# Attention probabilities of batch 0: turned by way of HBM and VectorE instead of on TensorE

## The reference

```python
xn = layernorm(x)
q, k, v = split(xn @ w_qkv.T + b_qkv)
probs = softmax(q @ k.T / sqrt(512))          # 1024 x 1024 for each batch
s = (probs @ v) @ w_out.T + b_out
# gate: a mixture of 8 experts on the same xn, best 2 of 8 for each token
topk_vals, topk_idx = top_k(xn @ router_w + router_b, 2)
h = silu(xn @ expert_w[e] + expert_b[e])      # for the two chosen experts
g = silu(norm_w * rms_normalise(xn + (sum of weighted h) @ proj_w + proj_b))
out = x + s * g
```

## Time and profile before

| | |
|---|---|
| median of 3 runs | 507.1 us (506.06 to 507.46) |
| the profiled execution | 505.39 us, span of its instructions 503.7 us |
| TensorE, VectorE, ScalarE, GpSimd busy | 488.0, 299.7, 206.7, 202.6 us |
| granted TensorE clock | 0.999 of full speed |
| DMA | 104.22 MB, mean 207 GB/s |

### The profile page before, as it was taken

How to read it: one execution, slowest core, us unless ns; L and a number is a source line. 1 busy time by engine, 2 the same in 40 slices (tenths; PEclk the granted TensorE clock), 3 DMA queues, 4 the chain that set the end, 5 groups by cost and what they waited for, 6 DMA issues and landing times.

```text
span 503.7 us, 7293 instructions
## 1 busy us (share of the span) xinstructions
PE 488.0 (97%) x2234; PEld 397.2 (79%) x2235; DVE 299.7 (60%) x452; ACT 206.7 (41%) x300; POOL 202.6 (40%) x288
## 2 busy tenths in 40 slices
PE   4999999999999999799999999999999999999996
PEld 2678686888888888688888888878888888888884
DVE  2556252576422535688888889763676645667452
ACT  1166373142212333854444444323454362525550
POOL 3044310004887835860000000754477772466134
PEclk9999999999999999999999999999999999999999
DMA  7863999912688489998985666987253451331202
GB/s 261 303 231 145 379 384 366 394 43 84 220 310 298 159 248 285 307 272 247 287 219 189 188 202 181 311 287 276 65 148 114 150 175 62 116 95 62 84 33 94
DMA packets 68364, 104.22 MB, mean 207 GB/s; under 512 B 5728, under 2 KB 29808, under 8 KB 68336
## 3 DMA queue, kind: packets, MB, share of 16 engines
q1 hardware_dynamic: 55120, 67.13, 42.1%
q0 software_dynamic: 7360, 25.19, 14.6%
q10 hardware_dynamic: 5856, 11.54, 6.5%
HBM read 60.32 MB, written 43.52 MB: 206 GB/s over the span
## 4 chain that ended last, share of the span: by engine, by line
PE 90%; DMA 3%; issue 2%; ACT 2%; POOL 1%; DVE 1%; SPq 1%; ACTq 0%
PE ab L1451 20%; PE ab L1453 20%; PE ab L1452 20%; PE sc L1451 6%; PE sc L1453 6%; PE sc L1452 6%; PE tp L1457 4%; PE sc L1468 3%; DMA raw<-in_expert_w 2%; PE tp L1502 2%; DMA raw_o<-in_w_out_t 1%; PE sc L1531 1%; PE ab L1476 1%; ACT W L941 1%; PE sc L1534 1%
## 5 line engine op out<-in xcount | busy, mean ns | idle before, releaser
L720 POOL DMA_INDIRECT y<-y_scratch,pos x32 | 31.1, 972 | 107.2 <-DMA y_scratch<-yt_so 92.5
L1451 PE MATMUL ab<-W,st_h 128*128 x156 | 60.9, 390 | 2.7 <-DVE st_l L1189 2.7
L1453 PE MATMUL ab<-W,st_l 128*128 x156 | 60.7, 389 | 0.0
L1452 PE MATMUL ab<-W,st_h 128*128 x156 | 60.7, 389 | 0.0
L703 POOL DMA_INDIRECT rows_scratch<-xb,pos x32 | 31.2, 976 | 52.4 <-DVEq L1185 44.2
L1451 PE MATMUL sc<-xt_h,t_h 128*128 128x512 f32 x128 | 50.3, 393 | 0.0
L1453 PE MATMUL sc<-xt_h,t_l 128*128 128x512 f32 x128 | 50.0, 390 | 0.0
L1452 PE MATMUL sc<-xt_l,t_h 128*128 128x512 f32 x128 | 49.8, 389 | 0.0
L932 ACT CAST st_h<-tp 128x512 fp32r<-128x512 f32 x39 | 22.9, 588 | 42.8 <-PE ab L1453 34.1
L1245 DVE TENSOR_REDUCE small<-sc 128x1 f32<-128x1024 f32 x16 | 19.6, 1224 | 29.8 <-PE sc L1453 25.4
L1451 PEld LDWEIGHTS ab<-W,st_h 128*128 128x128 f32 x156 | 29.3, 188 | 9.6 <-issue 3.5
(11 more groups left out here) (261 smaller groups left out, 1219.0 us busy)
## 6 DMA issues: line engine op xcount, KB each, us to landing
rows_scratch<-xn ACTq DMA_DIRECT2D x3, 3328.0 KB, 19.3
xb<-in_expert_w POOLq DMA_DIRECT2D x6, 1024.0 KB
xn<-rows_scratch SPq DMA_DIRECT2D x48, 128.0 KB, 3.0
xg<-rows_scratch SPq DMA_DIRECT2D x44, 128.0 KB
y_scratch<-yt_own SPq DMA_DIRECT2D x20, 256.0 KB, 2.6
y_scratch<-yt_so SPq DMA_DIRECT2D x19, 256.0 KB, 2.8
rows_scratch<-xs SPq DMA_DIRECT2D x16, 256.0 KB, 6.0
xb<-rows_scratch SPq DMA_DIRECT2D x16, 256.0 KB, 6.2
```

The costliest lines, as they stand in the source:

```text
L720: pool.indirect_dma_start(y[:, q, :], None, y_d, bass.IndirectOffsetOnAxis(pos[:, GB * s + p:GB * s + p + 1], 0))\
L1451: nc.tensor.matmul(dst, lh, rh, start=start, stop=False)
L1452: nc.tensor.matmul(dst, lh, rl, start=False, stop=False)
L1453: return nc.tensor.matmul(dst, ll, rh, start=False, stop=stop)
```

## The change

For the tiles 0 to 6 of batch 0 the eight transposes on TensorE go. ScalarE writes exp with the columns in another order, to one of three buffers in turn (`prob`, and memory of `xn` or `yt_own`, which are idle then). SP stores the 128 x 1024 tile (512 KB) to `p_scratch` in HBM (`store_prob`), waits for it to land, and loads it back with four DMAs of 128 KB in another order of rows (`load_prob`). VectorE turns 32 x 32 blocks of it into `tp` with two transposes (`p_turn`). Tile 7 is still turned on TensorE.

Around that, the queues are written out in a new order. TensorE makes four blocks of scores before the first attention block, the key weights of the second half follow the first attention block, and from then on an attention block is three tiles behind its scores. VectorE reads attention results and row maxima ahead of turns in its loop. The positions are computed before `texp`, which has its own semaphore `assigned`. SP asks for the raw weights of experts 3 and 4 one behind the other after the last scores, ahead of the pair loads; ScalarE casts expert 3 before the last `pt_split` and expert 4 before `g_split(0)`; the projection's raw weights are asked for later.

```diff
+    p_d = nc.dram_tensor("p_scratch", (GB, P, S), F32).ap()
+    p_q = p_d.rearrange("j (r s) (a f) -> j a s r f", r=4, a=4)
...
+        probs = tuple(prob[:, :] if j % 2 == 0 else xn_flat if j < QB else yt_flat for j in range(GB))
+        quarters = tuple(xs[:, 2 * n:2 * n + 2, :].rearrange("p a n -> p (a n)") for n in range(2))
...
+            def store_prob(j):
+                sp.wait_ge(exp_done, 2 + j + 1)
+                sp.dma_start(p_d[j], probs[j], max_dma_last_dim=4 * D).then_inc(p_out[j % 2], 16)
+
+            def load_prob(j):
+
+                sp.wait_ge(p_out[j % 2], 16 * (j // 2 + 1))
+                if j >= 2:
+                    sp.wait_ge(p_turned, j - 1)
+                for a in range(4):
+                    sp.dma_start(quarters[j % 2][32 * a:32 * (a + 1), :].rearrange("p (r f) -> p r f", r=4),
+                                 p_q[j, a, :, :, :]).then_inc(p_in[j % 2], 16)
...
+            sp.wait_ge(t_done, G)
+            for j in range(QB):
+                store_prob(j)
+                load_prob(j)
+            store_s(0)
+            for g in range(GB, GB + 4):
+                load_to_send(g)
+            for j in (QB, QB + 1):
+                store_prob(j)
+                load_prob(j)
+                store_s(j - 3)
+                for g in range(GB + 4 + 2 * (j - QB), GB + 6 + 2 * (j - QB)):
+                    load_to_send(g)
+            store_prob(GB - 2)
+            load_prob(GB - 2)
+            store_s(3)
+
+            sp.wait_ge(s_done, GB)
+            load_raw(sp, 3)
+            load_raw(sp, 4)
+            for g in range(GB):
+                sp.wait_ge(sent[g], 64)
+            load_pair(0, 0)
+            store_s(4)
+            load_pair(2, 1)
+            load_bias(0)
+            load_bias(1)
+            store_s(5)
+            load_next(4, 0)
+            load_bias(2)
+            load_bias(3)
+            store_s(6)
+            store_s(7)
+            load_next(6, 1)
...
+            def pt_split(j):
+                if j < GB - 1:
+                    act.wait_ge(p_turned, j + 1)
+                else:
+                    act.wait_ge(ptr_done, 1)
+                if j >= 2:
+                    act.wait_ge(ab_full, U["a", 0, j - 2] + 1)
...
+            def exp_0(j):
+                act.wait_ge(mx, j + 1)
+                if j >= 2:
+                    act.wait_ge(p_out[j % 2], 16 * (j // 2))
+                out, whole = probs[j], sc[:, j % 2, :, :].rearrange("p m n -> p (m n)")
+                if j < GB - 1:
+                    out = out.rearrange("p (a c q) -> p c a q", a=4, q=32)
+                    whole = whole.rearrange("p (c a q) -> p c a q", a=4, q=32)
...
+            act.wait_ge(zero_in, 48)
+            exp_0(1)
+            early_high(0)
+            pt_split(0)
+            exp_0(2)
+            exp_0(3)
+            early_high(1)
+            t_hi(0, 1, 0)
+            t_hi(0, 1, 1)
+            pt_split(1)
+            t_hi(0, 1, 2)
+            t_hi(0, 1, 3)
+            pt_split(2)
+            exp_0(4)
+            early_high(2)
+            pt_split(3)
+            exp_0(5)
+            pt_split(4)
+            exp_0(6)
+            pt_split(5)
+            exp_0(7)
+            early_high(3)
+            pt_split(6)
+
+            w_high(0)
+            w_high(1)
+            pt_split(7)
...
+            w_high(2)
+            w_high(3)
             g_split(0, 0, True)
             g_split(1, 1, True)
...
+            def p_turn(j):
+
+                dve.wait_ge(p_in[j % 2], 64 * (j // 2 + 1))
+                dve.wait_ge(pt_lo, j)
+                back = quarters[j % 2].rearrange("p (r c q) -> p c r q", r=4, q=32)
+                for h in range(2):
+                    last = vec.transpose(tp[:, h, :, :].rearrange("p c (r s) -> p c r s", r=4),
+                                         back[:, h * KC:(h + 1) * KC, :, :])
+                last.then_inc(p_turned, 1)
...
+            row_max(1)
+            next(routing)
+            p_turn(0)
+            row_max(2)
+            pt_low(0)
+            next(routing)
+            next(routing, None)
+            row_max(3)
+            p_turn(1)
+            attn_out(0)
+            t_lo(0, 1, 0)
+            t_lo(0, 1, 1)
+            pt_low(1)
+            p_turn(2)
+            t_lo(0, 1, 2)
+            t_lo(0, 1, 3)
+            pt_low(2)
+            p_turn(3)
+            row_max(4)
+            for j in range(3, GB - 2):
+                attn_out(j - 2)
+                pt_low(j)
+                row_max(j + 2)
+                p_turn(j + 1)
+            attn_out(GB - 4)
+            pt_low(GB - 2)
+            attn_out(GB - 3)
+            pt_low(GB - 1)
...
+            scores(0, 0)
+            count_chosen()
+            for j in range(1, QB):
+                scores(0, j)
+            attend_tile(0)
+            for n in range(KC):
+                key_weights(0, 1, n)
+            for j in range(QB, GB):
+                scores(0, j)
+                attend_tile(j - 3)
+            attend_tile(GB - 3)
+
+            pe.wait_ge(exp_done, 2 + GB)
+            pe.wait_ge(pt_lo, GB - 1)
+            transpose_tile(yt_flat[:, 0:KC * P], 0)
+            transpose_tile(yt_flat[:, KC * P:2 * KC * P], 1).then_inc(ptr_done, 1)
+            attend_tile(GB - 2)
+            attend_tile(GB - 1)
```

More of the change, by code:

```diff
@@ L546, in store_y @@
+            load_pair(0, 0)
[10 more added lines that the diff above has]
+            load_next(6, 1)
+            for k in range(4, E):
+                load_bias(k)
             def store_y(i, h):
@@ L897, in early_high @@
                 nc.scalar.copy(W[:, e, 0, :, :], wraw[:, k % 2, :, :]).then_inc(e_hi, 1)
[L899 to L919, removed]
-                    if i == 0 and j == 0:
-                        act.wait_ge(gate_d, 1)
-                        nc.scalar.activation(small[:, 10, :], small[:, 9, :], ACT.Exp).then_inc(gate_e, 1)
-                pt_split(QB - 1)
@@ new lines, in _ @@
+            for n in range(1, KC):
+                t_hi(0, 0, n)
+            exp_0(0)
+            act.wait_ge(gate_d, 1)
+            nc.scalar.activation(small[:, 10, :], small[:, 9, :], ACT.Exp).then_inc(gate_e, 1)
+            act.wait_ge(zero_in, 48)
[9 more added lines that the diff above has]
+            t_hi(0, 1, 2)
@@ new lines, in pt_low, with attn_out @@
+            def pt_low(j):
+                dve.wait_ge(pt_hi, j + 1)
+                vec.tensor_tensor(pt_l[:, j % 2, :, :], tp[:, :, :, :].rearrange("p a c n -> p (a c) n"),
+                                  pt_h[:, j % 2, :, :], ALU.subtract).then_inc(pt_lo, 1)
+            def attn_out(j):
+                at = 4 + j % QB
+                dve.wait_ge(ab_full, U["a", 0, j] + 1)
+                link(vec.reciprocal(small[:, at, 3:4], small[:, at, 2:3]))
+                dve.wait_ge(so_st[j % 2], 16 * (j // 2) + 16)
+                vec.scalar_tensor_tensor(so[:, j % 2, :], bank(("a", 0, j)), small[:, at, 3:4], sbias[:, :],
+                                         ALU.mult, ALU.add).then_inc(ab_read, 1)
@@ L1305, in add_bias @@
+            turn(0, 0, 0, True)
+            turn(1, 1, 0, True)
+            g_low(0, 0)
+            g_low(1, 1)
+            attn_out(GB - 2)
+            attn_out(GB - 1)
+            turn(2, 2, 0)
+            turn(3, 3, 0)
             def add_bias(i, h, first=False):
```

168 lines of the change are left out of this document (45 added, 123 removed).

## The result

The changed kernel takes 513.3 us (median of 4 runs, 511.9 to 515.2) against 506.7 for the kernel before on the same chip (506.1 to 507.5): ratio 1.0112, 95% interval 1.0075 to 1.015. It is 1.1% slower; 500.7 was forecast. The profiled execution took 515.2, the slowest of the four, and has a span of 513.4 us against 503.7. A ratio is always to the kernel before, timed beside the other on the same chip; it is an estimate from all their executions and not the quotient of the two medians, from which it differs by up to 0.3%.

A forecast was written before the change was run, and what follows sets the result against it. TensorE, busy 488.0 of 503.7 us, was taken as the bound. Seven turnings (6.4) and the expert stall (3.2) gained, less a new 3.2 us stall, gave -6.4: 500.7 us against the median 507.1; range 497.0 to 505.0.

The forecast's parts named there:

- seven turnings at 0.92: TensorE before the experts: seven of eight probability turnings go, each 0.92 us, 6.4 us in all.
- tile 0's round trip: First tile's store to HBM and reload with idle DMA engines: 7.7 us, data at 110.9, no stall at A0.
- L + 4.2: Last turning (tile 7) starts 4.2 us after the last scatter lands; at 184.9, a stall of 3.2 us.
- 7 for the store: Tile 5's probability store to HBM in full queues takes 7 us, so its data come at 171.
- No stall from these: Tiles 1 and 5 return from HBM in time; tile 5 at 171, its `pt_low` wanted at 176.
- 4.2 to landing: Last scatter's time to land after its issue, taken from row group 7 with a weight load beside it: 4.2 us.
- I take the 3.2 us as gained: Stall at the fourth expert tile goes, since raw weights 3 and 4 are asked for earlier: 3.2 us.
- rival (b): Expert stall moves, the next pair load still behind store 7: 3 us lost at fourth to sixth tile, 503.9; chance 0.15.
- I let the shift stand to the end: Behind 211 us TensorE waits for nothing, so the gain of 6.4 us lasts to the kernel's end.
- rival (d): Full queues land the last scatter late; the kernel loses from 187.1, and at 190 takes 510.0 us; chance 0.13.
- Order: Experiments' theory: three placements in the queues cost the time, and cost nothing when moved.
- volume: Experiments' theory: DMA engines are full from 140 us on, each added megabyte delays later transfers, moves only decide which.

The follow-up runs named there:

- Experiment 4: Changed kernel with the raw weights of experts 3 and 4 asked for behind the scatter wait and first pair load, casts later: 509.7 us, ratio 1.0033.
- experiment 3: Changed kernel with rows 14 and 15 asked for ahead of tile 5's reload and `pt_split(6)` ahead of `early_high(3)`: 506.7 us, ratio 0.9997.
- experiment 1: Changed kernel with the rows of scatter groups 14 and 15 asked for ahead of tile 5's reload: 509.8 us, ratio 1.0032.
- experiment 2: Changed kernel with ScalarE's `pt_split(6)` ahead of the cast `early_high(3)`: 512.6 us, ratio 1.0121.
- experiment 6: Kernel of experiment 3 with the biases of experts 4 to 7 asked for ahead of `store_s(6)`: 506.2 us, ratio 0.9978.
- experiment 5: Kernel of experiment 3 with the projection's raw weights issued before `w_high(4)`, as in the kernel before: 505.4 us, ratio 0.9981.
- experiment 7: Kernel of experiment 3 with the moves of experiment 5 and experiment 6 together: 506.7 us, ratio 0.9998.
- experiment 8: Kernel of experiment 7 with `store_s(5)` ahead of `load_pair(2, 1)` and two bias loads: 508.1 us, ratio 1.0017.

## Why the prediction was wrong

Right: seven turnings at 0.92 and TensorE ready at 181.93 (forecast 181.7). So was tile 0's round trip, where the DMA engines were idle. SP's queue and VectorE in the changed kernel:

```profile
103.48 0.38 SPq L530 DMA_DIRECT2D p_scratch<-prob  x1
106.23 1.75 SPq L538 DMA_DIRECT2D xs<-p_scratch  x4
```

```profile
110.78 1.32 DVE L1321 STREAM_TRANSPOSE tp<-xs 128x512 f32<-128x512 f32 x2 [0.84 <-DMA xs<-p_scratch]
```

2.75 us for the store where 3.3 were taken, data at 110.8 for 110.9, no wait at A0; GpSimd began at 117.94 (119.3). The place and the rule of the stall, L + 4.2, were right as well: L, the landing of the last scatter, was 186.7 and the turning began at 190.97.

**The step that failed first is the size of L: 186.7, not 180.7.** It has two mis-sized terms, both DMA durations in full queues:

- "7 for the store": it took 11.5. The data of tile 5 still came in time (VectorE turned it at 169.06, 171 was forecast), which is why the step ended in "No stall from these". That looked only at the tile. Behind the store stood the rows of groups 14 and 15, asked for at 166.3 instead of 163, and GpSimd was 4.8 us late instead of 1. The last scatter's issue ended at 178.7, not 176.5: 2.2 us.
- "4.2 to landing", from a scatter with one weight load beside it: 7.9 from the end of its issue. 3.7 us. Experiment 4 took the 2 MB away, and it was 3.6; but experiment 3 had them and it was 4.8, so the 2 MB are part of the cause and not shown to be all of it. The prediction's full queue did have these 2 MB; it had them 7 us sooner, at 171.

And a second wait lay hidden behind L, that of tile 6 for its own reload (5.1 to 8.9 us), which no step of the prediction had: it set the turning in experiments 1, 2 and 6.

L was inside its stated bounds (177.5 to 187), but the range of the time, 497.0 to 505.0, did not follow them: L = 186.7 alone gives 500.7 + 6.0 = 506.7. Three more steps failed:

- **The clock was never priced**: 2.6 us behind the 9.0 us wait. With it the experts start at 205.34 and not 196.7.
- **"I take the 3.2 us as gained"**: the stall didn't go but moved, by the mechanism of rival (b), one pair later. The load was that of a pair issued at 214 us, with the projection's raw weights beside it (214.54), and the stage lost 4.6 us in this execution against 3.2 before.
- **"I let the shift stand to the end"**: the wait of 1.6 us for `v_l` and 1.2 us at the end came behind 211, where nothing was expected. Such a wait for `v_l`, of 0.3 to 1.6 us, is in every kernel here with seven tiles by HBM and in none of the three others; why, no run shows.

Together 8.6 + 4.6 + 1.5 + 1.2 make the 16 us between the forecast span of 497.3 us (503.7 - 6.4) and the measured 513.4. Rival (b) and a stall at rival (d)'s break-even had 0.15 and 0.13 as exclusive cases, and came together. The DMA engines were full at both (0.97 from 175 to 215 us, 1.02 from 215 to 225), but a common cause is not shown: half the bytes took most of the first stall and left the second.

**Order or volume?** Both, for the stall ahead of the turning. Medians in us, with the ratios:

| | all bytes | half of the probabilities' bytes |
|---|---|---|
| the changed kernel's orders | 513.3 (1.0112) | 507.1 (0.999) |
| rows and split first, projection's weights back | 505.4 (0.9981) | 503.0 (0.9908) |

By the ratios, since the four were timed on more than one chip: good orders are worth 1.3% (6.7 us) with all bytes and 0.8% (4.2) with half; the bytes 1.2% (6.2) in the bad orders and 0.7% (3.7) in the good. Each of the four is clear of noise. That each covers part of what the other does, 0.5%, is not. In the expert stage Order fell: four moves (experiments 5 to 8) changed where the wait was, and gave 505.4, 506.2, 506.7 and 508.1 us from a base of 506.7. One reload took 5.1 us in one execution and 8.9 in another, with the same instructions ahead of it (experiment 6 beside 3); a new order of issues does not take that away by itself. Left open: which of the stage's own 2 MB of bias rows, 1 MB of projection weights or stores one would have to drop; that was not tried.

The rule weighed in the prediction, the Trainium skill's "VectorE: DVE Perf Modes", Rules for kernel authors, to turn 128 x 128 tiles on TensorE: by it no route should have won. Seven tiles by HBM lost 1.1%, and four, with better orders, won 0.9% against the kernel before, which turned all eight on TensorE. There the measurement differs from the rule: with TensorE busy for 97% of the span, the windows and experiments point to the room in the DMA engines, and to what stands in line behind the new transfers, as what decides.

## What to carry to other kernels

Before sending a step through HBM, add its bytes window by window to the busy share of the DMA engines, and use it only where there is room: four tiles in the roomy stretch gave 0.9%; seven cost 1.1% in the first orders and gave nothing measurable (ratio 0.9981) in good ones. In an in-order queue, price a slow transfer by what is queued behind its wait, not only by when its own data are wanted. And where TensorE is the bound, a stall has a tail of slow matmuls; take it into the price, and do not give stalls that can come together chances as exclusive cases. When the range of the time is set, carry each term's own bounds through to it.

## What was not expected of the hardware

- VectorE's two transposes of a probability tile took 1.32 us together, and the same two of an expert's rows 2.06 to 2.11 in this kernel and in the earlier trace rows. Shape and output are alike; what differs is the input's order, elements side by side for the first (`q` last) and every fourth for the second. No run changes that alone, so it is the likely cause and not a shown one.
- A `TENSOR_TENSOR` on one column takes 0.16 us, but 1.89 and 1.75 at two places. VectorE and GpSimd in the changed kernel:

```profile
119.78 1.89 DVE L1311 TENSOR_TENSOR small<-small,logits 128x1 f32<-128x1 f32 x1
...
130.68 1.32 DVE L1321 STREAM_TRANSPOSE tp<-xs 128x512 f32<-128x512 f32 x2
```

```profile
120.36 1.29 POOL L729 TENSOR_TENSOR W<-xb,W 128x512 fp32r<-128x512 f32 x1
...
131.56 1.30 POOL L729 TENSOR_TENSOR W<-xb,W 128x512 fp32r<-128x512 f32 x1
```

  The first ends at 121.67, just when GpSimd's operation does (121.65); the transposes ran into one of GpSimd's at 131.56 and neither got longer. The Trainium skill, "SBUF — State Buffer", Who interferes with whom, says that a VectorE instruction with two SBUF inputs contends with a GpSimd instruction that reads SBUF, and one with a single input, outside the modes that use two ports, doesn't; both rows agree. It cost nothing that shows here.
- A 512 KB store landed in 2.75 us with idle DMA engines and in 11.5 when they were full (busy share 0.89 from 140 to 175 us, and 1.02 at 387 GB/s while it was on its way): four times, not the two that were allowed for.
